# Two scaled weights, two token blocks and the first top-16 selection placed anew in a two-layer transformer kernel

## What is computed

```python
# layer 0: modulated by nine rows made from cond_1024
m = silu(mod) @ w_ada + b_ada                       # shifts, scales and gates: sh, sc, g
h = ln(x) * (1 + sc_msa) + sh_msa
x = x + self_attn_in_windows_of_128(h) * g_msa      # 16 heads of 16, tokens rolled by 64
h = ln(x) * (1 + sc_mca) + sh_mca
scores = q @ k.T / 4                                # against 154 context rows
top_s, top_i = top_k(scores, 16)                    # softmax over the 16 largest alone
x = x + (softmax(top_s) @ v[top_i] @ w_co + b_co) * g_mca
h = ln(x) * (1 + sc_mlp) + sh_mlp
x = x + ((silu(a) * b) @ w_m2 + b_m2) * g_mlp       # a, b = halves of h @ w_m1 + b_m1
# layer 1: full self attention over 1024 tokens, masked attention to the context, gelu MLP,
# each with a layer norm before it and a row t_emb @ tp_w added after it
```

## Time and profile before

| | us |
|---|---|
| median of 3 executions | 1518.57 (1518.34 to 1521.01) |
| the profiled execution | 1521.19 |
| its span in the trace | 1519.4 |
| mean granted PE clock in it | 0.954 |

### The profile page before, as it was taken

How to read it: one execution, slowest core, us unless ns; L and a number is a source line. 1 busy time by engine, 2 the same in 40 slices (tenths; PEclk the granted TensorE clock), 3 DMA queues, 4 the chain that set the end, 5 groups by cost and what they waited for, 6 DMA issues and landing times.

```text
span 1519.4 us, 25438 instructions
## 1 busy us (share of the span) xinstructions
PE 1379.1 (91%) x9100; PEld 691.2 (45%) x9100; DVE 918.1 (60%) x2815; ACT 713.3 (47%) x1454; POOL 342.0 (23%) x377
## 2 busy tenths in 40 slices
PE   7999887779889977999899999999999999988998
PEld 4467554444544544353233333333333335544675
DVE  3555487987787788675465666667676436650220
ACT  2255454647347345304644465555656674544221
POOL 1011167775555567000000000000000010010120
PEclk9899988879979988999999999999999999999999
DMA  5100002000000000000002000000000000000000
GB/s 189 50 22 26 20 18 99 22 2 1 1 15 2 1 28 1 27 1 1 1 2 69 2 1 2 1 2 1 2 12 1 2 2 2 13 3 3 14 18 28
DMA packets 22093, 26.74 MB, mean 18 GB/s; under 512 B 4205, under 2 KB 19635, under 8 KB 21709
## 3 DMA queue, kind: packets, MB, share of 16 engines
q1 hardware_dynamic: 21059, 25.03, 5.1%
q10 hardware_dynamic: 909, 0.10, 0.0%
HBM read 21.58 MB, written 3.08 MB: 16 GB/s over the span
## 4 chain that ended last, share of the span: by engine, by line
PE 66%; DVE 9%; issue 3%; ACT 3%; POOL 2%; DMA 1%; ACTq 0%; SPq 0%; POOLq 0%; DVEq 0%
PE bank L1076 24%; PE bank L1033 11%; PE bank L1116 8%; PE bank L1048 7%; PE bank L1012 3%; PE bank L991 3%; DVE x_hat L1495 2%; PE bank L1140 2%; PE bank L970 1%; PE bank L1159 1%; DVE left L1550 1%; PE bank L1018 1%; DVE left L1557 1%; DVE part_max L1522 1%; DVE top L1547 1%
## 5 line engine op out<-in xcount | busy, mean ns | idle before, releaser
L1306 ACT ACTIVATE pr<-bank 128x512 f32<-128x512 f32 x656 | 353.4, 598 | 289.4 <-PE bank L1076 276.2
L1522 DVE TENSOR_REDUCE part_max<-bank 128x1 f32<-128x512 f32 x512 | 327.0, 684 | 180.6 <-PE bank L1076 180.1
L1076 PE MATMUL bank<-slot 32*128 32x512 f32 (+1 forms) x3072 | 385.5, 521 | 10.4 <-ACT pr L1306 6.1
L1076 PEld LDWEIGHTS bank<-slot 32*128 32x128 f32 x3072 | 160.6, 186 | 210.3 <-issue 159.9
L1572 POOL TENSOR_SCALAR var_eps<-mean_var 128x4 f32<-128x4 f32 x24 | 5.6, 232 | 920.2 <-DVE mean_var L1486 920.2
L1628 POOL TENSOR_SCALAR left<-left 128x308 f32<-128x308 f32 x128 | 125.3, 979 | 105.2 <-ACT exp_all L1328 50.8
L1116 PE MATMUL bank<-pr,v 128*17 128x512 f32 x1024 | 135.3, 600 | 0.2
L1033 PE MATMUL bank<-h_t,w_m 128*128 128x512 f32 x256 | 130.7, 637 | 4.4 <-DVE o_all L1466 3.2
L1630 POOL TENSOR_TENSOR probs<-left,exp_all 128x308 f32<-128x308 f32 x128 | 107.4, 839 | 10.7
L1547 DVE MAX8 top<-bank 128x8 f32<-128x154 f32 x256 | 69.4, 312 | 50.0 <-PE bank L1140 39.0
L1328 ACT ACTIVATE exp_all<-bank,neg 128x154 f32<-128x154 f32 x256 | 85.7, 387 | 11.2 <-DVE left L1550 6.8
(11 more groups left out here) (140 smaller groups left out, 1775.6 us busy)
## 6 DMA issues: line engine op xcount, KB each, us to landing
w_m<-in_L_xcond_w_m SPq DMA_DIRECT2D x1, 2048.0 KB, 8.4
w_m<-in_L_xcond_w_m SPq DMA_DIRECT2D x2, 1024.0 KB, 8.1
w<-in_L_xcond_w SPq DMA_DIRECT2D x2, 1024.0 KB, 6.4
w_ada<-in_L_xcond_w_ada SPq DMA_DIRECT2D x1, 1792.0 KB, 10.6
x_sb<-in_x SPq DMA_DIRECT2D x6, 256.0 KB, 6.6
res_row<-rows_dram SPq DMA_DIRECT2D x12, 128.0 KB, 3.4
out_x<-x_sb SPq DMA_DIRECT2D x6, 256.0 KB, 2.1
wa<-in_L_xcond_w_qkv SPq DMA_DIRECT2D x1, 768.0 KB, 7.0
```

What stands on the lines that cost most here:

```text
L1076: last = nc.tensor.matmul(g.bank(*tile)[:, into], left, right, start=True, stop=True)
L1306: nc.scalar.activation(m.pr[:, u % NPR, :], g.bank("s", gi, i)[:, :], ACT.Exp).then_inc(g.free("s", gi, i), 1)
L1522: nc.vector.tensor_reduce(m.part_max[:, slot, h * TB + i // 8, i // 4 % 2:i // 4 % 2 + 1], bank[:, :], axis=AX.X, op=ALU.max).then_inc(don ...
```

## The change

Five edits of the plan and one of a wait:

- In `topk_run` the scores of the first tile stand 9.0 and those of the second 4.0 earlier on the plan, and the two `c_top` of the first tile 9.0 earlier.
- `c_top` 0 waits for the end of group 5 rather than of group 7.
- In `first_slots` the first `x_hat` pair stands ahead of the statistics of the second half.
- The blocks (1, 1) and (2, 0) come from `gap_slots` on fixed places between the score rounds, two places a round.
- `gate_m2` becomes four instructions over two row blocks each. Those of batch 0 stand at A2 + 9.3, 10.3, 11.3 and 12.3 steps (before: one at 8.5); those of batch 1 at the start of the third attention (before: A2 + 53.8 steps). What waited for the gate waits for its last part.
- In `rest`, the `x_hat` pair of block (4, 0, 1) stands behind the first `v` pair of block (4, 0, 0).

```diff
@@ topk_run
-                    plan.at(t0 - 0.8 * step, ("c_score", gi, t, 0), ("c_score", gi, t, 1), ("c_scores", gi, t))
+                    sooner = (9.0, 4.0)[u] if u < 2 else 0.0
+                    plan.at(t0 - 0.8 * step - sooner, ("c_score", gi, t, 0), ("c_score", gi, t, 1), ("c_scores", gi, t))
                     for hf in range(2):
                         t1 = t0 + 0.5 * hf * step
-                        plan.at(t1, ("c_top", gi, t, hf))
+                        plan.at(t1 - (sooner if u == 0 else 0.0), ("c_top", gi, t, hf))
@@ first_slots
-    first = [[("stats", s, b, 0), ("stats", s, b, 1), ("rstd", s, b, 0), ("stats", s, b, 2), ("stats", s, b, 3), ("rstd", s, b, 1)],
-             x_hat(0), [("prep",), ("mcol", 0), ("mcol_add", 0)], turns(0), modulate(0) + x_hat(1), [qk(0, 0)], turns(1), [out(0, 0)], [qk(0, 2)],
+    first = [[("stats", s, b, 0), ("stats", s, b, 1), ("rstd", s, b, 0)] + x_hat(0) + [("stats", s, b, 2), ("stats", s, b, 3), ("rstd", s, b, 1)],
+             [("prep",), ("mcol", 0), ("mcol_add", 0)], turns(0), modulate(0) + x_hat(1), [qk(0, 0)], turns(1), [out(0, 0)], [qk(0, 2)],
@@ make_plan
-    plan.spread(token_slots(1, 1), T + 18, T + 3.9 * W)
+    between = lambda first, last, per: [T + (c + (0.62 + i) / per) * R for c in range(first, last) for i in range(per)]
+    plan.fill(joined([gap_slots(1, 1, n) for n in range(2)]), between(5, 15, 2), (0.2 * R, 0.3 * R))
-    plan.spread(token_slots(2, 0), T + 6.0 * W, T + 9.4 * W)
+    plan.fill(joined([gap_slots(2, 0, n, 1) for n in range(2)]), between(23, 33, 2), (0.2 * R, 0.3 * R))
-    plan.at(A2 + 8.5 * step, ("stash",), ("load_w", "m1"), ("load_w", "m2a"), ("gate_m2", 0))
+    plan.at(A2 + 8.5 * step, ("stash",), ("load_w", "m1"), ("load_w", "m2a"))
+    for part in range(4):
+        plan.at(A2 + (9.3 + part) * step, ("gate_m2", 0, part))
-    rest = [head1[0], tail0[3], head1[1], tail0[4], tail0[5], head1[2]] + tail1
+    rest = [head1[0], tail0[3], tail0[4], head1[1], tail0[5], head1[2]] + tail1
-    plan.at(A2 + 53.8 * step, ("load_row", 4), ("load_row", 5), ("load_out", 4), ("load_w", "m2b"), ("gate_m2", 1))
+    plan.at(A2 + 53.8 * step, ("load_row", 4), ("load_row", 5), ("load_out", 4), ("load_w", "m2b"))
     A3 = T + 0.1
+    for part in range(4):
+        plan.at(A3 + 0.1 + part, ("gate_m2", 1, part))
@@ tensor_program (and SP's load_gate in the same way)
-                    pe.wait_ge(m.m2_gated, plan.n("gate_m2", b) + 1)
+                    pe.wait_ge(m.m2_gated, plan.n("gate_m2", b, 3) + 1)
@@ vector_program
-                dve.wait_ge(*g.group_end(7))
+                dve.wait_ge(*g.group_end(5))
@@ gpsimd_program
-            b = step[1]
+            b, part = step[1:]
-            w = m.m2[:, :, :]
-            nc.gpsimd.tensor_tensor(w, w, m.gate_row[:, q % 2, :].unsqueeze(1).to_broadcast([P, HT, C]), ALU.mult).then_inc(m.m2_gated, 1)
+            w = m.m2[:, 2 * part:2 * part + 2, :]
+            nc.gpsimd.tensor_tensor(w, w, m.gate_row[:, q % 2, :].unsqueeze(1).to_broadcast([P, 2, C]), ALU.mult).then_inc(m.m2_gated, 1)
```

More of the change, by code:

```diff
@@ L1719, in sync_program @@
                 if second0:
-                    sp.wait_ge(m.m2_gated, plan.n("gate_m2", b0) + 1)
+                    sp.wait_ge(m.m2_gated, plan.n("gate_m2", b0, 3) + 1)
                 else:
```

## The result

The changed kernel takes 1500.9 us in the median of four executions (1497.7 to 1502.0); the kernel before took 1519.45 beside it (1518.3 to 1521.0). The ratio is 0.9868, 95% interval 0.9851 to 0.9884. So the change saves 18.6 to 23 us. The forecast was 1491, a gain of 27.8. The time lies in the wide range (1482 to 1505), but outside the forecast's own (1485 to 1497); it is the time of rival 1 (1500), and as near to that of rival 2 (1499), so the total alone does not tell which of the two was right.

The account below looks back on a forecast made before the run. PE, busy 91% of the span, was taken to bound the kernel, losing time to waits and its lower clock. Six gains summed to 27.8: 1521.2 became 1493.4, less 2.6 for the median, say 1491; own range 1485 to 1497, wide 1482 to 1505.

Parts of the forecast that it names:

- rival 1: Token blocks' steps only move their waits; B and C give 3 and 2, gain 19, 1500 us; chance 0.22.
- rival 2: Selection run takes back its gains as PE becomes late; D, E, F give 5 together, 1499 us; chance 0.13.
- A: At 12.5 us, the first x_hat fills DVE's wait for statistics input, removing PE's 0.99 idle: gain 1.0.
- B: First attention, block (1,1) in fixed places: PE's waits and slow matmuls behind them mostly go; gain 7, between 3 and 8.9.
- C: First attention's end, block (2,0) finished before the last rounds: a round covers each wait; gain 6.8, between 2 and 10.
- D: Start of the selection run: first halves run ahead of group 7's end; gain 2.5, between 0 and 4.
- E: First gate, in four later parts: POOL's transfer wait no longer stalls DVE and PE; gain 7.5, between 4.5 and 9.
- F: Second gate leaves the selection run, x_hat (4,0,1) goes behind qk_d, freeing v's bank 4.6 earlier; gain 3, between 0 and 5.
- Rival 4: From 198 to 615 us PE's granted clock falls, say 0.88 to 0.81, and the whole gain is gone; chance 0.03.

Follow-up runs that it names:

- e_front: Kernel before with edits A to D alone, both gates and the swap as before: 1514.3 against 1521.3 us, ratio 0.9949.
- e_block11: Kernel before with A and B alone (first x_hat ahead, block (1,1) in fixed places): ratio 0.9977, 3.5 us gained.
- e_two_blocks: Kernel before with A, B and C alone, first selection and gates as before: ratio 0.9962, 5.8 us gained.
- e_run: Kernel before with E and F alone, first attention as before: ratio 0.9906, 14.3 us gained.
- e_gate0_whole: Kernel before with the first gate still one instruction, at 12.3 steps instead of 8.5: ratio 0.9961, 5.9 us gained.
- e_swap: Kernel before with only x_hat (4,0,1) put behind the first v pair of (4,0,0), second gate whole in its old place: ratio 0.9955, 6.8 us gained.
- e_gate0_parts: Kernel before with the first gate in four parts at 9.3 to 12.3 steps, second gate in its old place: ratio 0.9966, 5.2 us gained.
- e_apart11: Changed kernel with one empty slot between dependent steps of block (1,1): ratio 0.9870 to the kernel before.
- e_gate0_later: Changed kernel with the first gate's parts at 20.8 to 26.8 steps and the next gate row's load behind them: ratio 0.9843 to the kernel before.
- e_again: The whole change measured once more against the kernel before: ratio 0.9848, 23.1 us gained.
- e_filler: Changed kernel with block (2,0) on places 23 to 35 rather than 23 to 33: ratio 0.9876 to the kernel before.

## Why the prediction was right or wrong

| | forecast | in the trace | by the runs |
|---|---|---|---|
| A first x_hat | 1.0 | 0.7 | with B |
| B block (1,1) | 7 | 5.1 | A and B 3.5 |
| C block (2,0) | 6.8 | 2.9 | 2.3 |
| D first selection | 2.5 | 1.6 | 2.0 |
| E first gate | 7.5 | 4.3 | 5.2 |
| F swap, second gate | 3 | 7.0 | 6.8 |
| sum | 27.8 | 21.6 | 19.8 |

The trace column is from the changed kernel's profiled execution. For A it is 12.53 to 11.79. For A and B it is 5.85: the fifth maxima go to be turned at 124.73 instead of 130.58, ahead of the first step of block (2,0). C is 8.74 at group 7's end, less that (one tile of selection scores, 0.79, now stands ahead of this end, and may be added). D is a lead of 10.3 at half 4, less 8.74; E from 10.3 at half 20 to 14.6 at half 32; F from 17.2 at half 108 to 24.2 at half 116. Over the same halves the lead grows by 1.2 in `e_front`, `e_block11` and `e_two_blocks`, which leave this place as it was, and by 5.5 in `e_run`, so a lead across an edit is good to about 1 us. Another 2.6 come between halves 32 and 108, where nothing was changed, and 0.7 goes back behind half 116. The last column is from ratios of medians, with intervals of 3 us or more on each; C and D are differences of two runs, so A to D sum to `e_front`'s 7.8, and F is the swap alone. E and F together gave 14.3 in `e_run`, where the two rows sum to 12.0.

The terms missed in both directions: A to D by 9.5 too much, E by 2.3 too much, F by 3.8 too little. That F made good a part of the rest was luck. In the prediction's sum all lower ends give 9.5 (1509) and not 10.5 (1508).

The two columns differ most at B, and a single trace misleads there. Four kernels have none of A to D, and at half 4 their profiled executions lead that of the kernel before by -0.6 (`e_run`), 1.7 (`e_gate0_whole`), 3.4 (`e_swap`) and 3.7 (`e_gate0_parts`). Measured against these four, A and B give 6.5, 4.1, 2.5 and 2.4 at the fifth maxima; the runs have 3.5, and no single one of these figures decides.

**A** is right: the wait of 0.99 is gone. The transposes come only 0.74 earlier, because the matmuls ahead of them began 0.39 later, when their weights landed.

**B** failed at two terms. The mechanism was right, the `h_t` waits are gone. But "I leave 1.9 for x_hat still being late once" was too little: the idle times left are 4.2, with 2.24 for x_hat of the second half, 0.92 for that of the first, which stayed, and 0.69 for rows that the `mtp` matmuls need. And the 1.7 for the slow `qk` group was counted as certain: of the five profiled kernels with the same instructions there, it is slow in three and at full speed in two (last section). The 0.4 on the round behind it is not the clock's, since that round takes 1.59 in either case. A chain on POOL that I had not followed, two gatings of output weights that wait for a transfer until 78.2, adds 0.3 in the changed kernel, 1.3 in `e_block11`, where they end at 82.35 and the statistics at 81.07, and 3.5 in `e_apart11` (80.79 and 77.29). Their row was not among those I read, because before the change nobody waited there.

**C** failed as a sum of idle times. The end without a filler was forecast well: 3.2 of `o_copy` waits against 0.81, 0.99 and 1.72, 3.5 together. But 1.5 for slow matmuls and one packed round was too little: x_hat of this block waits 1.53 at 148.7, which I had at nothing, and two score rounds take 2.34 instead of 1.17, at a granted clock of 1.00. Less 1.53, and less the 0.8 by which the two rounds exceed my 1.5, the 6.8 is 4.5. The other 1.6 to 2.2 us can't be put to rows.

**Rival 1** had said of B and C: they give 3 and 2, and the total is 1500. By the runs they gave about 2.5 and 2.3, and the time is 1501. That the total fits as well is in part chance, since D, E and F gave 14.0 and not 13. Its mechanism was right in kind, the waits move; the carrier that I had written, the bank of `v`, is large only in `e_apart11`. It had 0.22 of the chances, and should have had more.

**D** is right, if a little high (2.5 against 1.6 and 2.0): `c_top` 0 starts at 183.36, ahead of the last `pv` at 187.79, and the memset at 190.42, 1.56 behind group 7's end, with 1.5 forecast.

**E** failed at "following DVE: halves 20 and 21 no longer wait". That is true of the halves, but `x_sum` stands between them, and it waits 3.22 for a `y_mm`. Before, that `y_mm` ran under DVE's 6.92. So the lead grew by 6.0 and not 7.8 up to half 23, and 1.7 of it went back by half 32. The sign that I had named, no DVE wait above 2 us, was the right one to look for, and it failed. POOL's part of the step (1.51 of wait, 1.26 to 1.32 each, picks between) was right, and mattered less than I thought, by `e_gate0_whole` and `e_gate0_later`.

**F** failed the other way, at "with x_hat behind `qk_d`, the bank comes free 4.6 earlier". It comes free 6.7 earlier: the wait of 2.00, x_hat's 2.64, and one `c_top` of 2.05. The order came from the list of slots; the program's order has one more exchange, which the planner makes when it finds no free bank.

**Rival 2**, that D, E and F give 5 together, is wrong: they gave 14.0. What it describes does occur on a smaller scale, behind the first gate and in `e_front`. **Rival 4** is wrong too: from 198 to 615 us the granted clock is 0.91 in the changed kernel and 0.88 before. The stages behind the run keep their length: the last 859 us of the span hold 819.05 us of PE work, before 819.00.

## What to carry over

When a wait is taken away, walk each engine's queue from that point to the next step that is not ready, through the steps of other chains that stand between: here an `x_sum` between two selections, and, once the statistics come earlier still, a gating that waits for a transfer ahead of the rstd. A row that costs nobody anything before the change belongs to the rows to read, if its step stands ahead of one that is to come earlier. And where a planner sorts or exchanges steps, derive the new order from the program that it makes, not from the list that goes into it: the smallest edit here was worth more than twice its forecast for that reason.

## What the runs showed of the hardware

**The same program differs by 12 us on its own.** The kernel before took 1516.7 to 1529.1 us in 35 executions, and the time goes with the mean granted clock of PE: 0.958 in the fastest, 0.949 and 0.950 in the two slowest, correlation -0.86. The profiled kernels that begin with the same instructions show where it starts. Here is the stretch 15 to 45 us in the kernel before and in `e_swap`, which differ only from 500 us on:

```profile
15.00:45.00 30.00, 28.69 (x153) 16.88 (x154) 10.24 (x25) 8.98 (x15) 0.00 (x0) 0.89 0.28 103
```

```profile
15.00:45.00 30.00, 28.91 (x157) 16.99 (x157) 10.80 (x25) 8.86 (x15) 0.00 (x0) 0.94 0.28 103
```

The clock is 0.89 in the one and 0.94 in the other, with PE busy for 96% of the stretch in both. At the first transpose of maxima `e_swap` is 1.65 ahead (48.64 against 50.29), and 1.70 come at the `qk` group that the next paragraph shows, so that at half 4 it leads by 3.4 us that no edit of its own can have given. `e_run` is 0.6 behind there; its first matmul waits for its weights until 8.98, where that of the kernel before waits until 8.00. All profiled executions here have either 0.89 or 0.94 in this stretch, kernels with the same instructions among both. So what an experiment leads by ahead of its own edit says nothing, and a gain in a trace is best taken as the difference of lead across the edit. Why one execution has 0.89 and another 0.94 isn't shown.

**The same idle stretch is followed by either level of the clock.** Five profiled kernels have the same instructions up to the first `qk` of block (1,1), and the same idle time ahead of it. Eight matmuls took 5.37 in the kernel before, in `e_run` and in `e_gate0_whole`, and 3.67 in `e_swap` and `e_gate0_parts`. PE of `e_gate0_whole`, then of `e_gate0_parts`:

```profile
68.30 5.37 PE L1013 MATMUL bank<-h_t,wa 128*128 128x512 f32 x8 [2.70 <-ACT h_t L1249]
```

```profile
68.31 3.67 PE L1014 MATMUL bank<-h_t,wa 128*128 128x512 f32 x8 [2.70 <-ACT h_t L1250]
```

Elsewhere it is the same. Behind the wait for x_hat near 86 us, `pv` ran at full speed (1.07) after 2.24 in the changed kernel, 2.61 in `e_again` and 2.67 in `e_gate0_later`, and slowly after 2.44 in `e_two_blocks` (1.91) and 2.71 in `e_block11` (1.77). The first `v` of (4,0,0), behind an idle 2.81 or 2.82, took 3.43 in the changed kernel and 1.99 in `e_filler`. Behind the 3.00 of `e_apart11` the group was slow (3.57 against 1.99). What decides isn't shown. So a slow group that is seen once behind a wait of this length is not a price to be counted in full.

The prediction quoted the Trainium skill, "TensorE: Matmul & The Clock Gate", section "HAM oscillation — how this bites in real kernels", for bursts that start cold behind each idle stretch. That page describes a kernel whose waits are some 3 to 5 us each time, and the prediction carried it over to waits of 0.9 to 2.7. The runs here agree for some stretches of 2.4 to 3.0 us and not for others. By that rule the gain was to be 4 us larger than the sum; it was smaller.
